# A mixture-of-experts kernel: y is weighted on the chip and added into two sums in DRAM instead of being stored pick by pick

## The reference

```python
router_logits = x @ gate_w
probs = softmax(router_logits)
top_vals, top_idx = top_k(probs, 8)
top_vals = top_vals / sum(top_vals)
rw[token, top_idx] = top_vals            # zero elsewhere, (1024, 64)
g = einsum('th,ehi->tei', x, w_gate)     # h = 256, i = 96
u = einsum('th,ehi->tei', x, w_up)
h = silu(g) * u * rw[:, :, None]
out = einsum('tei,eih->th', h, w_down)
```

## Time and profile before

| | us |
|---|---|
| median of the runs shown (415.79, 416.84, 417.10) | 416.84 |
| the profiled execution, device time | 417.87 |
| its span, first to last instruction | 416.1 |
| PE busy in the span | 275.1 (66%) |
| DVE busy | 210.7 (51%) |
| POOL busy | 214.0 (51%) |
| ACT busy | 118.0 (28%) |

### The profile page before, as it was taken

The page is one execution under the profiler, slowest core; times in us unless marked ns, Lnnn a source line. Parts: engine busy times, 40 slices in busy tenths (PEclk is TensorE's granted clock), DMA queues, the critical chain, the costliest instruction groups (busy, mean ns, idle before and its releaser), DMA issues.

```text
span 416.1 us, 5526 instructions
## 1 busy us (share of the span) xinstructions
PE 275.1 (66%) x1546; PEld 230.9 (55%) x1546; DVE 210.7 (51%) x921; ACT 118.0 (28%) x265; POOL 214.0 (51%) x256
## 2 busy tenths in 40 slices
PE   5898177137801610000199999999999999951997
PEld 1335067037800500000189999889999889931886
DVE  0799999989386679000033433343433343340352
ACT  2264353316634500000023333333333333320000
POOL 2622112013267777777327777777777777771000
PEclk9999999557975555555589999999999999995899
DMA  4899995360013333333498888888888887226891
GB/s 132 312 352 306 318 310 192 91 190 2 1 63 113 126 126 127 126 127 138 148 243 267 273 270 277 271 264 274 261 273 269 269 270 229 74 73 234 325 305 64
DMA packets 47374, 84.12 MB, mean 202 GB/s; under 512 B 10453, under 2 KB 28249, under 8 KB 46320
## 3 DMA queue, kind: packets, MB, share of 16 engines
q1 hardware_dynamic: 38128, 64.87, 49.9%
q0 software_dynamic: 9216, 18.90, 13.0%
HBM read 48.07 MB, written 39.85 MB: 211 GB/s over the span
## 4 chain that ended last, share of the span: by engine, by line
PE 52%; DVE 18%; POOL 16%; issue 7%; DMA 4%; ACT 2%; SPq 1%; POOLq 1%; ACTq 0%
PE psum L715 20%; POOL expert_rows L478 14%; PE psum L724 13%; PE psum L770 7%; PE psum L704 5%; DVE work L995 5%; DVE top L991 5%; DVE stats L966 2%; PE psum L536 2%; PE psum L530 2%; DMA sim<-token_picks 1%; POOL token_picks L499 1%; PE psum L604 1%; DVE adj L1000 1%; DMA gu_w<-expert_rows 1%
## 5 line engine op out<-in xcount | busy, mean ns | idle before, releaser
L499 POOL DMA_INDIRECT token_picks<-down_w,target x126 | 117.3, 931 | 54.9 <-issue 41.1
L715 PE MATMUL psum<-gu_w,wgu 128*96 128x192 f32 x504 | 93.7, 329 | 0.0
L715 PEld LDWEIGHTS psum<-gu_w,wgu 128*96 128x96 f32 x504 | 78.0, 165 | 0.6 <-DVE gu_w L1203 0.2
L478 POOL DMA_INDIRECT expert_rows<-x_rows,place_at x64 | 62.4, 975 | 23.8 <-issue 23.8
L724 PE MATMUL psum<-proj_t,gu_w 96*96 96x256 f32 x252 | 64.8, 379 | 0.0
L927 ACT ACTIVATE gu_w<-psum 96x192 f32<-96x192 f32 x63 | 20.6, 326 | 130.0 <-PE psum L715 130.0
L1208 DVE TENSOR_TENSOR gu_w<-gu_w,psum 96x192 f32<-96x192 f32 x63 | 22.1, 350 | 67.1 <-ACT gu_w L927 67.1
L704 PE MATMUL psum<-ident,gu_w 96*128 96x96 f32 x108 | 14.1, 256 | 53.1 <-DMA gu_w<-expert_rows 53.1
L933 ACT COPY down_w<-psum 96x512 f32<-96x512 f32 x63 | 36.6, 581 | 33.9 <-PE psum L724 33.9
L724 PEld LDWEIGHTS psum<-proj_t,gu_w 96*96 96x96 f32 x252 | 41.1, 163 | 7.1 <-DVE gu_w L1208 0.4
L704 PEld LDWEIGHTS psum<-ident,gu_w 96*128 96x128 f32 x108 | 12.5, 148 | 57.6 <-DMA gu_w<-expert_rows 54.4
(11 more groups left out here) (177 smaller groups left out, 397.1 us busy)
## 6 DMA issues: line engine op xcount, KB each, us to landing
expert_rows<-empty_rows SPq DMA_DIRECT2D x1, 15360.0 KB, 69.3
wgu<-in_L_ffn_w_gate_up SPq DMA_DIRECT2D x65, 192.0 KB, 2.9
gu_w<-expert_rows SPq DMA_DIRECT2D x28, 240.0 KB, 4.2
proj_t<-in_L_ffn_w_down SPq DMA_DIRECT2D x65, 96.0 KB, 4.0
sim<-expert_rows SPq DMA_DIRECT2D x18, 240.0 KB, 4.3
work<-expert_rows SPq DMA_DIRECT2D x18, 240.0 KB, 4.2
gu_w<-in_L_ffn_gate_up_proj SPq DMA_DIRECT2D x4, 512.0 KB, 8.2
sim<-token_picks SPq DMA_DIRECT2D x2, 1024.0 KB, 4.9
```

The source lines that it names most:

```text
L478: pool.indirect_dma_start(rows_dram, bass.IndirectOffsetOnAxis(ap=place_at[:, t, k:k + 1], axis=0), x_rows[:, t, :], None).then_inc(placed ...
L499: pool.indirect_dma_start(picks_dram, bass.IndirectOffsetOnAxis(ap=target[0:SLOTS, e % T_RING, i:i + 1], axis=0), y_slots[0:SLOTS, n, i, : ...
L715: last = pe.matmul(psum[0:I1, 2 + e % 2, part * CAP:(part + 1) * CAP], wgu[:, n, k, part * I1:(part + 1) * I1], x_slots_t[:, e % 2, k, :], ...
```

## The change

Weights travel with the rows. A row now has 256+1+64 = 321 elements: its data, the number of its token, and its 64 router weights, which `router_weights` writes straight into it. So `router_weights(b)` stands ahead of `place_rows(b)`, and POOL waits for it. The pick numbers, `pick_weights` and `build_diag` go.

In the loop DVE copies the token numbers and, as one more operation, the 96x2 weights of the unit's own expert out of the rows. ACT writes y with these weights as its scale, in two operations instead of one. POOL's scatter adds y, by a DMA with `compute_op=add`, to one of two tables of sums in DRAM, for even and odd units. Because an add reads its destination and writes it later, each scatter waits until that of two units back, which went to the same table, has landed. An empty slot holds the number of a spare row behind the 1024 tokens, so all 192 rows of a unit are in bounds. SP clears the two tables ahead of the first weights.

At the end SP loads each table in two halves of four tiles (512 KB each), and PE adds them with two matmuls by the identity per tile, 16 in all. The first table is asked for before the last unit's scatter has landed.

On ACT the load of the Exp table stands ahead of `copy_logits(0)`, and `exp_logits(0)`, `(1)` ahead of the last two `evacuate_down`. `X_RING` is 9 instead of 10.

```diff
-X_RING = 10
+X_RING = 9
+SUMS = 2
-    ROW = D + NE
+    ROW = D + 1 + NE
...
+            for n in range(SUMS):
+                sp.dma_start(sums_dram[n].rearrange("(r p) d -> p r d", p=CLEAR_P),
+                             empty_rows[0:CLEAR_P, 0:1, 0:D].to_broadcast([CLEAR_P, (T + CAP) // CLEAR_P, D])).then_inc(sums_cleared, 16)
...
+            def load_sums(n):
+                for half in range(2):
+                    tiles = slice(half * NT // 2, (half + 1) * NT // 2)
+                    sp.dma_start(sums[n][:, tiles], sums_dram[n][0:T].rearrange("(t p) d -> p t d", p=P)[:, tiles]).then_inc(sums_landed[half][n], 16)
+
+            load_sums(1 - LAST_Y % SUMS)
             sp.wait_ge(scattered[LAST_Y], total_over * (16 * SUBS) + SCATTERED[LAST_Y])
             sp.sem_inc(over_begun, 1)
-            picks_f = picks_dram.rearrange("(t p k) d -> t p (k d)", p=P, k=TOP_K_EXPERTS)
-            for t in range(NT):
-                need(sp, picks_summed, t - K_RING + 1)
-                sp.dma_start(picks[t % K_RING], picks_f[t]).then_inc(picks_landed[t % K_RING], 16)
+            load_sums(LAST_Y % SUMS)
...
                         pool.wait_ge(place_ready, b + 1)
+                        pool.wait_ge(rw_ready, b + 1)
...
             def scatter(e):
                 n = e % Y_RING
                 pool.wait_ge(y_ready, e + 1)
+                need(pool, scattered[(e - SUMS) % Y_RING], 16 * SUBS * ((e - SUMS) // Y_RING + 1))
                 for i in range(SUBS):
-                    pool.indirect_dma_start(picks_dram, bass.IndirectOffsetOnAxis(ap=target[0:SLOTS, e % T_RING, i:i + 1], axis=0),
-                                            y_slots[0:SLOTS, n, i, :], None, bounds_check=T * TOP_K_EXPERTS - 1, oob_is_err=False).then_inc(scattered[n], 16)
+                    pool.indirect_dma_start(sums_dram[n % SUMS], bass.IndirectOffsetOnAxis(ap=target[0:SLOTS, e % T_RING, i:i + 1], axis=0),
+                                            y_slots[0:SLOTS, n, i, :], None, bounds_check=T + CAP - 1, oob_is_err=True, compute_op=ALU.add).then_inc(scattered[n], 16)
...
-            for t in range(NT):
-                pe.wait_ge(diag_ready, t + 1)
-                pe.wait_ge(picks_landed[t % K_RING], 16 * (t // K_RING + 1))
-                for k in range(TOP_K_EXPERTS):
-                    last = pe.matmul(psum[:, t, 0:D], diag[:, t % 2, k, :], picks[t % K_RING][:, k * D:(k + 1) * D],
-                                     start=k == 0, stop=k == TOP_K_EXPERTS - 1)
-                last.then_inc(picks_summed, 1)
+            for half in range(2):
+                for n in range(SUMS):
+                    pe.wait_ge(sums_landed[half][n], 16)
+                for t in range(half * NT // 2, (half + 1) * NT // 2):
+                    for n in range(SUMS):
+                        last = pe.matmul(psum[:, t, 0:D], ident[:], sums[n][:, t], start=n == 0, stop=n == SUMS - 1)
+                    last.then_inc(tokens_summed, 1)
...
             silu_and_up0(2 * NE0 - 1)
+            act.preload_act_table(ACT.Exp)
             copy_logits(0)
             copy_logits(1)
+            exp_logits(0)
+            exp_logits(1)
             evacuate_down(2 * NE0 - 2)
             evacuate_down(2 * NE0 - 1)
-            act.preload_act_table(ACT.Exp)
-            exp_logits(0)
-            exp_logits(1)
...
-                act.copy(y_slots[0:SLOTS, n].rearrange("p i d -> p (i d)"), psum[0:SLOTS, 4 + e % 2, 0:SUBS * D]).then_inc(y_ready, 1)
+                for i in range(SUBS):
+                    last = act.activation(y_slots[0:SLOTS, n, i], psum[0:SLOTS, 4 + e % 2, i * D:(i + 1) * D], ACT.Copy,
+                                          scale=slot_w[0:SLOTS, e % T_RING, i:i + 1])
+                last.then_inc(y_ready, 1)
...
-                for t in tiles:
-                    last = dve.tensor_tensor_scan(order[:, t], chosen[:, t], zeros[:], 0.0, ALU.add, ALU.add)
-                link(last)
-                for t in tiles:
-                    dve.tensor_scalar(x_rows[:, t, D:ROW].bitcast(U32), order[:, t], -1.0, token_end[:, t:t + 1], ALU.mult, ALU.add)
...
+            router_weights(0)
             place_rows(0)
+            router_weights(1)
             place_rows(1)
...
-                dve.tensor_copy(target[0:SLOTS, e % T_RING], x_slots[e % X_RING][0:SLOTS, :, D + e + 1].bitcast(U32))
+                dve.tensor_copy(target[0:SLOTS, e % T_RING], x_slots[e % X_RING][0:SLOTS, :, D].bitcast(U32))
+                dve.tensor_copy(slot_w[0:SLOTS, e % T_RING], x_slots[e % X_RING][0:SLOTS, :, D + e + 2])
```

More of the change, by code:

```diff
@@ L61, in gated_layers_kernel @@
     MAX_OVER = P // 2
+    CLEAR_P = P // 2
     rows_dram = nc.dram_tensor("expert_rows", [NE * T + CAP, ROW], F32, kind="Internal").ap()
-    picks_dram = nc.dram_tensor("token_picks", [T * TOP_K_EXPERTS, D], F32, kind="Internal").ap()
+    sums_dram = [nc.dram_tensor(f"token_sums{n}", [T + CAP, D], F32, kind="Internal").ap() for n in range(SUMS)]
     with ExitStack() as stack:
@@ L163, in gated_layers_kernel @@
         reuse = gu_w[:].rearrange("p e k n -> p (e k n)")
-        cuts = [0, 4 * SUBS * ROW]
+        cuts = [0, 3 * SUBS * ROW]
         for n in (2 * KC * CAP, 2 * CAP, 2 * CAP):
             cuts.append(cuts[-1] + n)
-        x_homes = [(reuse, n) for n in range(4)]
+        x_homes = [(reuse, n) for n in range(3)]
         for home in (sim, work):
@@ L177, in gated_layers_kernel @@
         y_slots = down_w[:].rearrange("p e i d -> p (e i d)").rearrange("p (n i d) -> p n i d", n=Y_RING, i=SUBS)
-        diag = xn_t[:].rearrange("p k t -> p (k t)").rearrange("p (n k j) -> p n k j", n=2, k=TOP_K_EXPERTS)
-        picks = [t[:].rearrange("p t s -> p (t s)") for t in (sim, work, adj, base)]
+        sums = [t[:].rearrange("p t s -> p (t s)").rearrange("p (t d) -> p t d", d=D) for t in (sim, work, adj, base)]
         psum = stack.enter_context(nc.psum_tensor("psum", [P, N_BANKS, BANK], F32))
@@ L209, in gated_layers_kernel @@
         over_begun = sem("over_begun")
-        picks_landed = [sem(f"picks_landed{n}") for n in range(K_RING)]
-        diag_ready, picks_summed = sem("diag_ready"), sem("picks_summed")
+        sums_cleared = sem("sums_cleared")
+        sums_landed = [[sem(f"sums_landed{half}_{n}") for n in range(SUMS)] for half in range(2)]
+        tokens_summed = sem("tokens_summed")
         out_ready, stored = sem("out_ready"), sem("stored")
@@ L946, in _ @@
                 act.wait_ge(scattered[LAST_Y], j * (16 * SUBS) + SCATTERED[LAST_Y])
-                act.copy(y_slots[0:SLOTS, LAST_Y].rearrange("p i d -> p (i d)"), psum[0:SLOTS, 4 + LAST_TWO, 0:SUBS * D]).then_inc(y_ready, 1)
+                for i in range(SUBS):
+                    last = act.activation(y_slots[0:SLOTS, LAST_Y, i], psum[0:SLOTS, 4 + LAST_TWO, i * D:(i + 1) * D], ACT.Copy,
+                                          scale=over_w[0:SLOTS, i:i + 1])
+                last.then_inc(y_ready, 1)
         @block.vector
@@ L1189, in _ @@
             dve.sem_inc(over_ready, 1)
-            router_weights(2)
-            router_weights(3)
-            for b in range(B):
-                pick_weights(b)
             total_over = load_over(dve)
@@ L1208, in up_times_silu1 @@
                 dve.tensor_tensor(h1_t[:, e % 2], silu1[:, e % 2], psum[0:I1, 2 + e % 2, CAP:2 * CAP], ALU.mult).then_inc(h_ready, 1)
-            def build_diag(t):
-                need(dve, picks_summed, t - 1)
-                for k in range(TOP_K_EXPERTS):
-                    last = dve.tensor_scalar(diag[:, t % 2, k, :], ident[:], pick_w[:, t, k:k + 1], None, ALU.mult)
-                last.then_inc(diag_ready, 1)
             copy_slots_t(0)
@@ L1226, in _ @@
                 dve.wait_ge(scattered[LAST_Y], j * (16 * SUBS) + SCATTERED[LAST_Y])
-                dve.tensor_tensor(over_target[0:SLOTS], x_slots[LAST_X][0:SLOTS, :, bass.ds(e + D, 1)].rearrange("p i a -> p (i a)").bitcast(U32),
-                                  over_void[0:SLOTS, :, bass.ds(j, 1)].rearrange("p i a -> p (i a)"), ALU.max).then_inc(over_target_ready, 1)
+                dve.tensor_copy(over_w[0:SLOTS], x_slots[LAST_X][0:SLOTS, :, bass.ds(e + D + 1, 1)].rearrange("p i a -> p (i a)"))
+                for i in range(SUBS):
+                    last = dve.scalar_tensor_tensor(out=over_target[0:SLOTS, i:i + 1], in0=x_slots[LAST_X][0:SLOTS, i, D:D + 1].bitcast(U32),
+                                                    scalar=spare_row[0:SLOTS, i:i + 1], in1=over_void[0:SLOTS, i, bass.ds(j, 1)],
+                                                    op0=ALU.min, op1=ALU.max)
+                last.then_inc(over_target_ready, 1)
                 dve.wait_ge(xt_filled, j + (UNITS + 1))
```

53 lines of the change are left out of this document (22 added, 31 removed).

## The result

The changed kernel takes **481.99 us** (median of 4 runs, 478.19 to 484.38), the kernel before 416.97 beside it (4 runs, 415.79 to 418.01): a ratio of 1.1552, 95% interval 1.147 to 1.1633. The prediction was 409, with 438 as the upper end. The mean distance of two units' scatters, called p as in the prediction, is 3.78 us instead of 2.50.

A forecast was written before the change was run, and what follows sets the result against it. PE's work was taken to bound the loop, after POOL's 64 row DMAs and before a tail with 30.50 us of PE sums. Span 237.0 + 63 periods of 2.72 gave 408.4, device 409; range 396 to 438, likeliest 403 to 416.

The forecast's parts named there:

- POOL's part of an adding DMA: Loop: reading the destination adds 0.135 us per scatter DMA, spacing 1.355, so 2.71 per unit on POOL.
- the landing: Loop: a scatter lands 2.25 us after POOL's part, bounds 1.38 to 3.7; the wait then gives 2.72 per unit.
- The front: Before the loop: POOL's first row DMA comes 1.26 us later, bounds 0.2 and 2.5.
- The clearing of the sums: SP's queue before the loop: 2.5 MB more to clear, +11 us for the first weight loads, hidden.
- The added copy on DVE: Loop: DVE's extra 0.17 us copy charged nothing; as a rival (0.03) it holds POOL, period 2.89, 420 us.
- Rows of 321 elements: Row DMAs: no change in descriptor counts; by the skill, row loads an estimated 8% longer, 0.07 us per unit.
- The tail: After the loop: PE's summation falls from 30.50 to 9.5 us; each 512 KB half table loads in 3.75.
- The landing fits: Rival (0.18): in the loop the add's read is hidden and landings take at most 2.0; 397 to 402 us.
- Late landing: Rival (0.28): in the loop adds land too late, from 2.5 us after POOL's part; 436 us at 3.1, 455 at 3.7.
- The engines fill up: Rival (0.12): in the loop loads and scatters fill the DMA engines, scatters 1.43 us per unit; period 2.92, 421 us.
- PE's clock: Loop: the clock might fall below 1.00 because PE has gaps; priced at nothing.
- The signs named ahead: Loop: PE gaps about 0.2 us per unit, through y_ready or POOL; POOL idle above 0.5 means landing above 2.7.

The follow-up runs named there:

- four_tables: The changed kernel with four tables of sums instead of two, so a scatter waits for that of four units back; 470.12 us, ratio 1.1256.
- plain_four: The changed kernel with plain writes instead of adds and four tables instead of two; 410.79 us, ratio 0.9867, in the third attempt.
- plain_sums: The changed kernel with plain writes instead of adds, keeping the wait for the landing of two units back; 426.28 us, ratio 1.0214.
- before_wait: The kernel before, its plain scatter made to wait for the landing of that of two units back; 442.01 us, ratio 1.0628, in the third attempt.
- split_tail: The kernel before with PE summing 5 of 8 picks, DVE the other 3, ACT building the diagonals, six pick slots instead of four; 406.77 us, ratio 0.9767.
- no_weight_loads: The changed kernel without weight loads in the loop, all units using the first eight experts' weights; 459.12 us, one run.
- skip_empty: The changed kernel with empty slots numbered out of bounds again, so the add skips them; 477.73 us, ratio 1.1433.

## Why the prediction was wrong, step by step

**The step that failed first: POOL's part of an adding DMA.** The prediction priced the read of the destination "as 96 further addresses", +0.135. It is +0.49, the same for 48 rows as for 96. The text named the upper bound rightly, "a second fixed part, which nothing in the trace resembles", and then left it out of the range. A second part as large as the first, 0.92-0.13 = 0.79, would have given 2 x (1.22+0.79) = 4.0 per unit; the truth, 3.42, lies inside that bound. An operation that the trace does not show had no reason to be near the low end. This step alone puts the time above the upper end of 438: the prediction's own sum with p = 3.42 gives 237.0+63 x 3.42+0.74 = 453, and `four_tables`, the add without the new wait, takes 470.12 with its longer end.

**The second: the landing.** Taken was L = 2.25 after POOL's part, with the add's read in it. Beside the loads even a plain scatter takes 3.5 to 3.6 from its start where a wait slows the loop, so 2.6 to 2.7 after POOL's part, and 4.1, so 3.2, in `plain_four`, which keeps the engines busy 0.93 of the time; in the quiet tail it was 1.38. The adding one takes 4.6 in the change, at 0.92: also 3.2 after POOL's part, and up to 4.3. At that load the add's read doesn't show in the landing; in the quiet part it does, with 1.9 after POOL's part against 1.4. The rival of a late landing had this (3.7 as its end), and it was priced by the right sum, but with the DMA of 1.05. With the measured terms the prediction's formula gives for the median (1.71+1.41+3.2+0.83)/2 = 3.58 and for the long ones (L = 4.2) 4.08; the mean, 3.78, lies between. The formula itself misses that landings scatter: an early one gives nothing back below POOL's 3.42. The Trainium skill, DMA: Bandwidth & Descriptors, section "Latency and other measured facts", puts an access to HBM at 0.2 us on average and 2 us at high load, and calls the way to the memory and back the main part of a DMA's fixed cost. That the quiet 1.38 became 2.6 beside the loads agrees with it in kind. The prediction allowed for the queueing one small load at most (2.3 us), and took less.

**The sum.** Predicted span 408.4, measured 480.5, +72.1:

| term | predicted | measured |
|---|---|---|
| first scatter starts | 216.2 | 217.5 |
| p, times 63 | 2.72: 171.4 | 3.78: 238.0 |
| first to second DMA of the last unit | 1.355 | 1.71 |
| its DMA and landing | 3.30 | 6.51 |
| load of half a table | 3.75 | 3.93 |
| PE's sums | 9.5 | 10.04 |
| around these and the last store | 2.8 | 2.8 |

66.6 of the 72.1 are p. How it divides: the add alone accounts for 59 of the loop's 81 us over 2.50 per unit. The wait on top of it, 63 x (3.78-3.43), is 22. The two are not independent terms: POOL's longer part is also in the chain of the landings.

**Right.** *The front*: POOL's first row DMA, predicted for 117.1, is at 117.13 in the timeline, and the last at 201.91, +1.05 for +1.26. About 1.5 us more pass up to the first scatter; ACT's second scaled copy is 0.25 of them, the rest stays open. The clearing of the sums is hidden, as said.

```profile
117.13 1.26 POOL L488 DMA_INDIRECT expert_rows<-x_rows,place_at  x1 [6.29 <-DVE place_at L1108]
```

*The added copy on DVE* was charged at nothing against the rule of the Trainium skill (SBUF — State Buffer, "SBUF: two separate sides"), which would have had 11 us. The measurement decides: of the 126 copies of 96x2 that DVE makes in the loop of `plain_sums` (two per unit), 87 lie wholly inside one of the 126 plain scatters, and none of these took over 0.946 us. It is DVE's copies that get longer there: inside a scatter 0.32 and 0.26 in the median, outside one 0.17 and 0.16. Why is open, since in the kernel before the copy takes 0.17 in either place. The 16 operations of 128x128 do hold a DMA: 2.82 in `before_wait`, where DVE builds the diagonals in the middle of the last scatters. In `split_tail`, where ACT builds them, the same DMA (371.44) is back to the usual length, and so are the two that lie beside ACT's diagonals, which fits the rule's naming of VectorE:

```profile
371.44 0.91 POOL L501 DMA_INDIRECT token_picks<-down_w,target  x1 [0.30 <-issue]
372.30 3.03 ACT L954 ACTIVATE xn_t<-ident,pick_w 128x128 f32<-128x128 f32 x10
373.37 0.92 POOL L512 DMA_INDIRECT token_picks<-down_w,over_target  x1 [1.01 <-ACT down_w L949]
374.59 0.92 POOL L512 DMA_INDIRECT token_picks<-down_w,over_target  x1 [0.30 <-issue]
```

*Rows of 321 elements*: the loads of rows land in 4.2 us in the median before and after, those of weights in 2.9; the 8% that the prediction estimated from the Trainium skill (DMA: Bandwidth & Descriptors, "How a descriptor splits into AXI transactions") don't show in it. The DMA issues (KB each, median us to landing), of the kernel before and then of the changed one:

```profile
gu_w<-expert_rows SPq DMA_DIRECT2D x28, 240.0 KB, 4.2
```

```profile
wgu<-in_L_ffn_w_gate_up SPq DMA_DIRECT2D x65, 192.0 KB, 2.9
gu_w<-expert_rows SPq DMA_DIRECT2D x22, 240.8 KB, 4.2
```

*The tail*: PE's 9.5 were 10.04 at a mean clock of 0.71. The first table was to be loaded under the last scatter. It was, and that last landing took 6.51 us beside it, where 3.3 was predicted; the scatter before it, with no table's load beside it, took 3.5. The loads of the loop are not the cause, since `no_weight_loads`, with 3.6 in the median of its loop, ends in the same way (chain of waits):

```profile
434.28 6.90 DMA token_sums<-down_w,over_target
```

In `plain_sums` SP asked for the table at 399.9, ahead of both last scatters (400.5 and 401.7), and both took 4.9 to 5.1. So each late one lies beside the table's load, and each early one ahead of it; a version that loads the table later was not tried.

**The rivals.** *The landing fits* (0.18): no; a landing had 2.07 us, and needs 2.6 without any add. *Late landing* (0.28): its mechanism is there, and its sign; its highest time, 455, fell short by POOL's 0.36 per unit. *The engines fill up* (0.12): its term, 1.43 us of the engines per unit for scatters, was near, and still it didn't set p. The page's row for POOL's DMA queue, of `four_tables` and then of `plain_four` at 410.79 (packets, MB, share of the span):

```profile
q0 software_dynamic: 17408, 23.11, 27.1%
```

```profile
q0 software_dynamic: 9216, 23.11, 15.9%
```

That is 126.9 us against 65.0 of mean engine time, so 0.48 more for each of 128 adding DMAs. If the placing of rows before the loop is put at 85 us x 0.34 = 29, the plain scatters take (65-29)/64 = 0.56 per unit, and with the add an estimated 1.5. In the loop `four_tables` keeps the engines busy 0.99 of the time, `no_weight_loads` 0.74 (table of stretches, in this order):

```profile
300.00:350.00 50.00, 39.07 (x235) 32.03 (x235) 14.56 (x60) 14.74 (x43) 40.91 (x30) 1.00 0.99 220
```

```profile
300.00:350.00 50.00, 39.63 (x232) 31.45 (x231) 14.19 (x60) 15.76 (x45) 40.98 (x30) 1.00 0.74 131
```

Both have p = 3.43, so POOL sets it, and not the engines: with a quarter of their work gone nothing gets faster. But at 0.99 they stand right behind. How much a cheaper part of POOL would give before the engines bind was not tried on an undisturbed chip. *PE's clock*, unpriced: 0.97 in the loop, and PE idles a quarter of it. That this costs nothing in the loop is argued from that and was not tried. *The signs named ahead*: PE's gaps came, but through DVE and ACT's order and not through `y_ready`; and POOL's idle time put down to a DMA was only 23.2 us, 0.37 per unit, under the 0.5 that was to tell L above 2.7, though L was 3.2. ACT waits for the same landings (151.6 us), and POOL's own work, 3.42 per unit, goes on meanwhile.

## What to carry to other kernels

Before an engine is given an operation that the trace does not show, take the whole of its known fixed cost as the bound for the new one, and keep that bound in the range; where the engine has 0.06 us of room per unit, as POOL had here, what exceeds that room is multiplied by the number of units. A landing measured in a quiet part of the trace is a lower bound only: beside the loads of the loop (227 GB/s in `before_wait`) it was nearly double (2.6 for 1.38), and more at 294 GB/s in `plain_four` (3.2), so a wait for a landing should reach back as many units as that takes. And an end that is worth improving (here 30.5 us of summation) can be shortened where it stands, as `split_tail` does by giving each engine a share, without a price on every unit of the loop.

## What the runs showed of the hardware that was not expected

- An indirect DMA of 96 rows that adds costs POOL 1.41 us, the plain one 0.92. 48 rows that are added: 1.34. The surcharge is the same where the empty slots, a third of all, are out of bounds (1.41 in `skip_empty`).
- It also leaves more packets. Plain: 9216 for 192 DMAs (64 of rows, 128 scatters) is 48 each. With the add 17408-64 x 48 = 14336, 112 for each of 128, and the engines' time for one rises by 0.48 us. With 48 rows in 126 of the DMAs there are 11360, which is 48 fewer in each: one packet for each row. Whether POOL's surcharge comes from these packets is open, since it does not fall with them.
- A scatter's landing, from the start of POOL's part: plain 2.29 in the quiet tail, 3.5 to 4.1 in the loop; adding 3.3 quiet, 4.4 to 4.8 in the loop (medians).
- From a landing to the start of the DMA on POOL that waited for it 0.83 us pass, to ACT's next operation 0.09 (306.09 to 306.92 and 306.18).
